# A two-layer decoder on one core: key banks of the first context projection doubled, the folding of layer 1's weights moved to the experts' stage, the stream's row factors made one stage earlier

## The chip, the cores and the metric

The kernel runs on one core of a Trainium2 chip. Its five engines are named as in the profile: PE (TensorE; its weight loads have a row of their own, PEld), DVE (VectorE), ACT (ScalarE), POOL (GpSimd) and SP (SyncE, which here only issues DMAs; its queue is SPq). The metric is the device time of the core in microseconds; less is better.

## The reference

Two decoder layers over a stream `x` of 32 sequences, 112 rows, 256 columns, and a context of 32 times 375 rows of 192 columns:

```
layer 0: x = LN_out(self_attention(LN(x))) * g + b + residual terms     (8 heads of 64)
         x = x + cross_attention(LN(x), context)                        (16 heads of 16, with output projection)
         x = x + top-2-of-8 experts(LN(x))                              (gelu, 1024 hidden)
layer 1: x = x + gated attention(LN(LN(x)*ln_g + ln_b))                 (one head of 128, gate of 512)
         x = x + cross_attention(LN(x)*g + b, LN(context)*tg + tb)      (16 heads of 16)
         x = x + top-2-of-8 experts(x)                                  (squared relu, 512 hidden)
```

Layer 1 normalises with a scale and a shift per column (`ln_g`, `ln_b`, `norm_g`, `norm_b`, `tnorm_g`, `tnorm_b`). The kernel doesn't apply them to the data: it multiplies the scale into the rows of the weights behind the normalisation, and adds the shift times the weights to the bias. This is called the folding. It needs the weights once, at any time before layer 1.

## The kernel before

Seven stages run one after the other, with a barrier of all engines between two of them. Each engine has its own program, and the order in it is written out by hand; engines wait for one another by counting semaphores (`pe.wait_ge(k_low, ...)`). The stages are `self_attention`, `project_context`, `cross_attention` (layer 0), `experts` (layer 0), `gated_attention`, `cross_attention` (layer 1) and `experts` (layer 1).

**project_context.** For each of the 32 contexts (index i) the functions of `context_writer` make the keys and values of layer 0. SP loads the transposed context into one of four slots `ctxT` (three DMAs, L893 and L895). PE multiplies (`project`, L953 to L962): two starts of the values (L953), the keys of two halves m = 0, 1 (L956, L958) and the rest of the values (L959, L960, L962). The keys go to the two PSUM banks `KEYS`, one for each m. ACT copies each key bank into `halves`, rounded (L996, counted by `k_high`), DVE writes the rest that the rounding lost beside it (L1037, counted by `k_low`); ACT and DVE each copy a part of the values into `v` (L1001, L1042). SP stores `halves` (L905, after `k_low`) and `v` (L909), and then loads context i + 4. `halves` and `v` have two slots; ACT and DVE wait for the store of context i - 2 before they write. The values have two pairs of PSUM banks, but the keys have one pair: before the keys of context i, PE waits until DVE has read those of context i - 1 (`pe.wait_ge(k_low, ONE + 2 * i)`).

Beside this the stage does other work, at fixed i. ACT finishes the self-attention's output of two sequences at each of i = 2 to 17 (`move`: four activations, L1090 and L1092). DVE, after its part of i = 4, 6, ..., 18, works on four sequences (`finish`: three adds or products of 1024 columns, L1126 to L1128, and four sets of row statistics, L254). At i = 22 (`ASK`) DVE makes the mean and the row factor of the context for layer 1 (`make_rstd_dve`, 14 small operations with one square root on ACT between them). PE does its part of the folding after context 6 (`fold_pe`: products of the shift with the weights, L339 to L356, into banks 0 and 1), and DVE its part at i = 22 behind the row factors (`fold_dve`: five additions to biases, L365 to L370, and nine products of weights, L373 to L380).

**cross_attention, layer 0.** ACT first clears two slots of `qP` (`clear`, L1426), DVE makes the mean and row factor of the stream `x` (the same 14 operations, on 32 columns) and a tile of ones (L1519), and then for the first two sequences: DVE normalises (L1524), PE turns it (L1301), ACT copies (L1437), PE projects the query (L1307), DVE splits it (L1532 to L1539), SP stores it and loads it back (L1249, L1260), after which the scores (L1325) begin. Keys and values are loaded by L1235 and L1243.

**experts, layer 0.** First comes the routing: PE turns the rows and makes the gate's products, DVE picks two experts for each row and works out the slot of each (a chain of small operations); for this PE counts with two products (L1801, L1802), and later adds up 128 one-hot products in four parts (L1809), each of which waits for DVE's `spread`. DVE reads the result off into the lists `came` and `goes` (L1990 to L2000), and POOL gathers the first rows (L1664). Then the tiles run, 31 of 256 slots and 4 of 128 (`tile`, PE L2103 and L2115; DVE only adds a bias, L2162, and scatters are POOL's). At last a stage part joins the experts' results to `x` and makes the keys and values of layer 1 with `context_writer` (tiles `d_...`; there PE turns the context itself, L938).

Of the kernel before, what the change touches and what calls it, by code (L numbers as in the profile page):

```python
# [20 lines left out]
P = 128  # L21
EPS = 1e-5
GROUP = 4
ONE = 1
# [30 lines left out]
def decoder(nc, d, out):  # L55
# [21 lines left out]
    with ctx:  # L77
# [256 lines left out]
        def fold_pe(pe, wide_ready, folded_ps):  # L334

            pe.wait_ge(later, later_n)
            pe.wait_ge(wide_ready, KD + 2)
            for k in range(KD):
                pe.matmul(bank[1][0:T, :], w.ln_b_wide[:, k, :], w.in_[:, k, 512:1024],  # L339
                          start=(k == 0), stop=(k == KD - 1))  # L340
            for m in range(9):
                for k in range(KD):
                    pe.matmul(bank[0][:, m:m + 1], w.in_[:, k, m * P:(m + 1) * P],
                              w.ln_gb[:, KD + k:KD + k + 1], start=(k == 0), stop=(k == KD - 1))

            for m in range(KD):
                for k in range(KD):
                    pe.matmul(bank[0][:, 16 + m:17 + m], xa[1].wqh[:, k, m, :],
                              xa[1].gb[:, KD + k:KD + k + 1], start=(k == 0), stop=(k == KD - 1))
                for k in range(2):  # L350
                    n = P if k == 0 else C1
                    pe.matmul(bank[0][:, 32 + m:33 + m], xa[1].wkh[0:n, k, m, :],
                              xa[1].gb[0:n, 6 + k:7 + k], start=(k == 0), stop=(k == 1))
            for k in range(2):
                n = P if k == 0 else C1
                last = pe.matmul(bank[0][0:T, D:2 * D], xa[1].b_wide[0:n, 2 + k, 0:T], xa[1].wv[0:n, k, :],  # L356
# [3 lines left out]
        FOLDS = 6 + 4 * KD  # L360

        def fold_dve(dve, fold_chain):

            fold = Chain(dve, fold_chain, 0, FOLDS)
            fold(dve.tensor_tensor(w.b_in_v[:], w.b_in_v[:], bank[1][0:T, :], ALU.add))  # L365
            fold(dve.tensor_tensor(w.b_in_u[:], w.b_in_u[:], bank[0][:, 0:9], ALU.add))
            fold(dve.scalar_tensor_tensor(out=xa[1].bq[:], in0=xa[1].bq[:], scalar=XD ** -0.5,
                                          in1=bank[0][:, 16:16 + KD], op0=ALU.mult, op1=ALU.add))
            fold(dve.tensor_tensor(xa[1].bk[:], xa[1].bk[:], bank[0][:, 32:32 + KD], ALU.add))
            fold(dve.tensor_tensor(xa[1].post[:], xa[1].post[:], bank[0][0:T, D:2 * D], ALU.add))  # L370

            for k in range(KD):
                fold(dve.tensor_scalar(w.in_[:, k, :], w.in_[:, k, :], w.ln_gb[:, k:k + 1], None, ALU.mult))  # L373
                n = P if k == 0 else C1
                wqh, wkh, wv = (xa[1].wqh[:, k].rearrange("c h n -> c (h n)"),
                                xa[1].wkh[:, k].rearrange("c h n -> c (h n)"), xa[1].wv[0:n, k, :])
                fold(dve.tensor_scalar(wqh, wqh, xa[1].gb[:, k:k + 1], None, ALU.mult))
                fold(dve.tensor_scalar(wkh, wkh, xa[1].gb[:, 4 + k:5 + k], None, ALU.mult))
                fold(dve.tensor_scalar(wv, wv, xa[1].gb[0:n, 4 + k:5 + k], None, ALU.mult))
            fold(dve.tensor_scalar(xa[1].wv_twice[:], xa[1].wv_twice[:], xa[1].gb[:, 5:6], None, ALU.mult))  # L380
            fold.close()
# [74 lines left out]
        env.fold_wide, env.fold_pe, env.fold_dve, env.FOLDS = fold_wide, fold_pe, fold_dve, FOLDS  # L456
# [395 lines left out]
def context_writer(e, layer, first, n, tag, sb):  # L852
# [6 lines left out]
    TURN, KEYS = (bank[0], bank[1]), (bank[2], bank[3])  # L859
    V02, V1 = (bank[4], bank[5]), (bank[6], bank[7])  # L860
# [22 lines left out]
    c = Parts()  # L883

# [57 lines left out]
    def project(pe, i):  # L942
# [11 lines left out]
        pe.wait_ge(k_low, ONE + 2 * i)  # L954
        for m, rows in enumerate((low, top)):
            pe.matmul(KEYS[m][:, 0:NKV], a.wkh[rows, 1, m, :], cT[rows, 1, :], start=True, stop=False)  # L956
        for m in range(2):
            pe.matmul(KEYS[m][:, 0:NKV], a.wkh[:, 0, m, :], cT[:, 0, :], start=False, stop=True).then_inc(k_ps, 1)  # L958
# [25 lines left out]
    def scalar(act, i):  # L984
# [7 lines left out]
        for m in range(2):  # L992
# [3 lines left out]
            act.activation(halves[:, i % 2, m, 0, 0:NKV], KEYS[m][:, 0:NKV], ACT.Identity,  # L996
# [1544 lines left out]
```

## Time and profile before

| | us |
|---|---|
| time, median of 3 runs | 2876.21 (2872.34 to 2879.39) |
| the profiled execution's own time | 2876.75 |
| span of the profiled execution | 2874.9 |
| of it `project_context`, from the end of self-attention to the first operation of cross-attention | 384.6 to 573.0 |
| of it the start of cross-attention, to the first scores | 573.0 to 590.5 |
| of it the routing of layer 0 | 1048.0 to 1129.3 |
| PE busy in the span | 2575.8 (90%) |

A row of the timeline gives start, duration, engine, line, operation, output and input, a count, and in brackets the idle time of the engine before it with what ended it. A matmul of 32-bit numbers is two instructions in the trace, so `x4` in a row is two matmuls of the program. A window's row gives for each engine the busy time, then the granted TensorE clock (1.00 is 2.4 GHz, 0.50 is 1.2 GHz), the busy share of the DMA engines and the rate. That share can come out somewhat above 1.

### The profile page before, as it was taken

What the parts mean: (1) busy time and instruction counts of PE and PEld (TensorE: products, weight loads), DVE (VectorE), ACT (ScalarE), POOL (GpSimd) and SP (SyncE); (2) the same over time, 40 slices, a digit from 0 to 9 for tenths busy, and PEclk for the clock granted to TensorE, in tenths of its full rate; (3) what the DMA queues carried; (4) which work ended last, traced back from release to release, by engine and by line L of the source; (5) the groups of instructions that cost most, each with busy time, mean ns of one, the idle gap of its engine ahead of it and who ended that gap; (6) DMA issues with size and microseconds to landing.
All of it is one profiled execution on the core that took longest, in us unless ns stands there. A gap on an engine that the chain in (4) does not pass through costs nothing. (4 is left out here: it accounts for less than half of the span.)

```text
span 2874.9 us, 57394 instructions
## 1 busy us (share of the span) xinstructions
PE 2575.8 (90%) x19210; PEld 2037.6 (71%) x19210; DVE 1529.1 (53%) x3357; ACT 1122.1 (39%) x2398; POOL 599.6 (21%) x652
## 2 busy tenths in 40 slices
PE   7999979789999975999999799899799999579992
PEld 4555555478888864888888566566688888468881
DVE  6777756456766664000000288455577777643334
ACT  2333345345555540333333244222455555312220
POOL 0000000023333310222222100000233333125542
PEclk9999999989999987999999899899899999779995
DMA  5110157777777732555555699000588888226666
GB/s 146 45 29 25 29 174 263 273 194 192 186 189 190 188 93 74 192 192 192 192 192 188 191 343 308 29 1 1 136 204 209 204 203 206 73 93 210 206 208 188
DMA packets 288417, 463.56 MB, mean 161 GB/s; under 512 B 75074, under 2 KB 216228, under 8 KB 288276
## 3 DMA queue, kind: packets, MB, share of 16 engines
q1 hardware_dynamic: 271508, 412.45, 50.3%
q0 software_dynamic: 16768, 49.30, 5.3%
q8 instruction: 80, 1.31, 0.2%
q14 instruction: 61, 0.50, 0.1%
HBM read 342.60 MB, written 119.02 MB: 161 GB/s over the span
## 5 line engine op out<-in xcount | busy, mean ns | idle before, releaser
L1444 ACT ACTIVATE x_probT<-banks 125x448 f32<-125x448 f32 x768 | 418.0, 544 | 382.9 <-PE banks L1341 372.8
L1544 DVE TENSOR_REDUCE x_neg_max<-banks 112x2 f32<-112x750 f32 x512 | 455.4, 930 | 93.4 <-PE banks L1325 93.4
L2103 PE MATMUL banks<-f_xT,f_w 128*128 128x256 f32 (+1 forms) x1680 | 369.9, 377 | 21.8 <-DMA f_b<-in_L_ffn_b 8.6
L2103 PEld LDWEIGHTS banks<-f_xT,f_w 128*128 128x128 f32 x1680 | 310.6, 197 | 74.9 <-issue 11.1
L1490 POOL TENSOR_TENSOR x_diag<-ident,x_neg_max 112x448 fp32r<-112x448 f32 x256 | 240.9, 941 | 581.6 <-DVE x_neg_max L1544 550.6
L2115 PE MATMUL banks<-f_w,f_hT 128*128 128x256 f32 x1584 | 355.8, 381 | 0.0
L1339 PE MATMUL banks<-x_diag,x_ones 112*125 112x448 f32 x768 | 324.0, 422 | 0.7 <-ACT x_probT L1444 0.6
L2115 PEld LDWEIGHTS banks<-f_w,f_hT 128*128 128x128 f32 x1584 | 297.7, 192 | 37.6
L1341 PEld LDWEIGHTS banks<-x_qP,x_kP 128*125 128x125 f32 x1536 | 290.5, 189 | 14.9
L1341 PE MATMUL banks<-x_qP,x_kP 128*125 128x224 f32 x1536 | 290.6, 271 | 0.0
L2162 DVE TENSOR_TENSOR f_y<-banks,f_b 128x256 f32<-128x256 f32 x66 | 25.1, 420 | 475.7 <-PE banks L2115 475.7
L1325 PE MATMUL banks<-x_kP,x_qP 128*112 128x376 f32 x1024 | 264.5, 341 | 9.4 <-DMA x_qP<-q_halves 8.6
L2055 POOL DMA_INDIRECT y_rows<-f_y,f_goes x132 | 131.4, 996 | 465.9 <-DVE f_y L2162 338.3
L2137 ACT ACTIVATE f_hT<-banks,f_b 128x256 f32<-128x256 f32 (+1 forms) x280 | 126.0, 461 | 220.2 <-PE banks L2103 202.7
L1357 PE MATMUL banks<-x_probT,x_v 125*32 125x112 f32 x6144 | 200.2, 263 | 0.8 <-ACT x_o4T L1452 0.8
L1339 PEld LDWEIGHTS banks<-x_diag,x_ones 112*125 112x125 f32 x768 | 143.6, 187 | 32.2 <-ACT x_probT L1444 22.0
L1357 PEld LDWEIGHTS banks<-x_probT,x_v 125*32 125x32 f32 x6144 | 138.6, 109 | 29.9 <-ACT x_o4T L1452 1.2
L1325 PEld LDWEIGHTS banks<-x_kP,x_qP 128*112 128x112 f32 x1024 | 147.1, 180 | 11.8 <-issue 9.1
L2046 POOL DMA_INDIRECT f_x_slots<-x_rows,f_came x124 | 121.6, 980 | 48.9 <-issue 36.6
L2140 ACT ACTIVATE f_hT<-banks 128x256 f32<-128x256 f32 (+1 forms) x140 | 51.9, 371 | 189.1 <-PE banks L2103 188.3
L2154 DVE TENSOR_TENSOR f_hT<-f_hT 128x256 f32<-128x256 f32 (+1 forms) x140 | 57.5, 411 | 88.7 <-ACT f_hT L2140 88.5
L1497 POOL TENSOR_TENSOR x_res<-x_res,x_post 112x256 f32 (+1 forms) x64 | 52.3, 818 | 223.8 <-DVE x_xn L1524 223.8
(331 smaller groups left out, 3789.1 us busy)
## 6 DMA issues: line engine op xcount, KB each, us to landing
x_kP<-k_halves SPq DMA_DIRECT2D x512, 188.0 KB, 3.6
f_w<-in_L_ffn_w SPq DMA_DIRECT2D x70, 1024.0 KB
f_w<-in_L_ffn_w SPq DMA_DIRECT2D x70, 512.0 KB
x_qP<-q_halves SPq DMA_DIRECT2D x512, 56.0 KB, 3.2
x_v<-v_rows SPq DMA_DIRECT2D x64, 408.0 KB, 3.2
k_halves<-p_halves SPq DMA_DIRECT2D x32, 752.0 KB, 4.5
k_halves<-f_d_halves SPq DMA_DIRECT2D x32, 752.0 KB, 6.4
q_halves<-x_q_halves SPq DMA_DIRECT2D x64, 224.0 KB, 2.3
```

The lines of the kernel that those rows point to most:

```text
L1325: last = pe.matmul(bank[2 * pair + k][0:T, 0:NKV + 1], qP[:, s, k, 2 * q + pair, :], kP[:, r, 2 * q + pair, :], start=True, stop=True)
L1339: pe.matmul(to, ones[:], diag[:, u % RING].rearrange("t h k -> t (h k)"), start=True, stop=False)
L1341: last = pe.matmul(to[:, 2 * pair * T:2 * (pair + 1) * T].rearrange("k (h t) -> k h t", t=T), kP[:, r, 2 * q + pair, keys], qP[:, s, :, 2 ...
L1357: last = pe.matmul(PV[j * VW:(j + 1) * VW, 0:T], v[0:KB, s % 2, at:at + VW], probT[:, u % 2, c, j, :], start=(c == 0), stop=(c == NJ - 1))
L1444: act.activation(probT[:, u % 2, c].rearrange("k h t -> k (h t)"), ST[i % 2][0:KB, 0:HU * T], ACT.Exp).then_inc(exp_done, 1)
L1490: pool.tensor_tensor(diag[:, u % RING], wide(ident[0:T, 0:T].unsqueeze(1), 1, HU), wide(mx[:, u % RING, :].unsqueeze(2), 2, T), ALU.mult). ...
L1544: dve.tensor_reduce(mx[:, u % RING, 2 * pair:2 * pair + 2], psum[0:T, 2 * pair:2 * pair + 2, 0:NKV], AX_X, ALU.max, negate=True).then_inc( ...
L2046: pool.indirect_dma_start(out=x_slots[:, n % 2, j, :], out_offset=None, in_=e.x_rows, in_offset=bass.IndirectOffsetOnAxis(ap=came[:, at:at ...
L2055: pool.indirect_dma_start(out=e.y_rows, out_offset=bass.IndirectOffsetOnAxis(ap=goes[:, at:at + 1], axis=0), in_=y[:, n % 2, j, :], in_off ...
L2103: last = pe.matmul(bank[1 + f % 3][:, 0:width], w1[:, r, k, f * P:(f + 1) * P], xT[:, r, k, 0:width], start=(k == 0), stop=(k == KD - 1))
L2115: last = pe.matmul(bank[4 + 2 * r + j][:, 0:D], hT[:, f, j * P:(j + 1) * P], w2[:, r, f, :], start=(f == 0), stop=(f == NF - 1))
L2137: act.activation(hT[:, f, 0:width], bank[1 + f % 3][:, 0:width], ACT.Gelu, bias=b1[:, r, f:f + 1]).then_inc(h_raw, 1)
```

## The change

Four things are done. (1) In layer 0's `context_writer` the keys use four banks, 0 to 3: context i takes one pair, context i + 1 the other, and PE waits for `k_low` of context i - 2 instead of i - 1. (2) `fold_pe` no longer runs in `project_context`; in the routing of layer 0 it stands between the counting products and the one-hot products and writes banks 1 and 2. (3) `fold_dve` is cut in two: the five additions to biases (`fold_biases`) stand at the end of DVE's routing program, and the nine products of weights (`fold_weight`) are put, two for each tile, ahead of DVE's work in tiles 30 to 34 of layer 0's experts. (4) The mean and row factor of the stream for cross-attention of layer 0 are made in `project_context` at i = 26 (`X_ASK`) and no longer at the start of cross-attention. POOL's `fold_wide` stays where it was.

```
     TURN, KEYS = (bank[0], bank[1]), (bank[2], bank[3])
+    if layer == 0:
+        KEYS = bank[0:4]
...
+    def keys_of(i, m):
+
+        return KEYS[(2 * i + m) % len(KEYS)][:, 0:NKV]
...
-        pe.wait_ge(k_low, ONE + 2 * i)
+        pe.wait_ge(k_low, ONE + least(2 * i + 2 - len(KEYS)))
         for m, rows in enumerate((low, top)):
-            pe.matmul(KEYS[m][:, 0:NKV], a.wkh[rows, 1, m, :], cT[rows, 1, :], start=True, stop=False)
+            pe.matmul(keys_of(i, m), a.wkh[rows, 1, m, :], cT[rows, 1, :], start=True, stop=False)
...
-        MOVE, FOLD, ASK = 2, 6, 22
+        MOVE, ASK, X_ASK = 2, 22, 26
...
                 for i in range(B):
                     c.tensor(pe, i)
-                    if i == FOLD:
-                        e.fold_pe(pe, wide_ready, folded_ps)
...
                     if i == ASK:
                         e.make_rstd_act(act, c_std, c_asked, ctmp)
+                    if i == X_ASK:
+                        e.make_rstd_act(act, x_std, x_asked, e.norm_tmp)
...
                         e.make_rstd_dve(dve, chain, c_std, c_asked, e.cmv, e.crstd[:], ctmp, False, e.cstat, e.DC)
-                        dve.wait_ge(folded_ps, 1)
-                        e.fold_dve(dve, fold_chain)
+                    if i == X_ASK:
+                        dve.wait_ge(rested, 3 * NG)
+                        chain = Chain(dve, x_chain)
+                        e.make_rstd_dve(dve, chain, x_std, x_asked, mv, rstd[:], e.norm_tmp, False, e.stat6)
...
-                chain = Chain(dve, pre)
-                e.make_rstd_dve(dve, chain, std_ready, std_asked, mv, rstd[:], e.norm_tmp, layer == 1, e.stat6)
+                if layer == 1:
+                    e.make_rstd_dve(dve, Chain(dve, pre), std_ready, std_asked, mv, rstd[:], e.norm_tmp, True,
+                                    e.stat6)
...
+        FOLD = (bank[1], bank[2])
...
                     pe.wait_ge(xT_ready, ONE + NG * KD)
+                    if layer == 0:
+                        e.fold_pe(pe, FOLD, fold_ps)
                     for n in range(2 * B):
...
                     link(dve.tensor_copy(goes[:], spare[:]))
+                    if layer == 0:
+                        dve.wait_ge(fold_ps, 1)
+                        e.fold_biases(dve, FOLD, Chain(dve, fold_chain))
...
                     width = halves(n) * P
+                    if layer == 0 and type(n) is int:
+                        for j in range(2 * (n - PAIRED + 1), min(e.SCALES, 2 * (n - PAIRED + 2))):
+                            e.fold_weight(dve, j, scale)
```

PE's program after context 6 of `project_context`, before (rows are instructions by line, output, input, shape and count; L953 is the first line of a context, the 128x1 products are the folding of shifts into biases):

```order
L962 MATMUL banks<-x_wv,p_ctxT 125x256 x2
L339 MATMUL banks<-w_in,w_ln_b_wide 112x512 x2
L343 MATMUL banks<-w_ln_gb,w_in 128x1 x18
L348 MATMUL banks<-x_gb,x_wq_by_head 128x1 x2
L352 MATMUL banks<-x_gb,x_wk_by_head 128x1 x2
L348 MATMUL banks<-x_gb,x_wq_by_head 128x1 x2
L352 MATMUL banks<-x_gb,x_wk_by_head 128x1 x2
L356 MATMUL banks<-x_wv,x_b_wide 112x256 x2
L953 MATMUL banks<-x_wv_twice,p_ctxT 125x256 x2
```

Now, in PE's program of the routing of layer 0 (L1821 and L1822 are the two counting products, L1831 the one-hot products; lines of the changed kernel):

```order
L1821 MATMUL banks<-f_both,f_before 112x256
L1822 MATMUL banks<-f_both,f_ones 112x256
L337 MATMUL banks<-w_in,w_ln_b_wide 112x512 x2
L341 MATMUL banks<-w_ln_gb,w_in 128x1 x18
L346 MATMUL banks<-x_gb,x_wq_by_head 128x1 x2
L350 MATMUL banks<-x_gb,x_wk_by_head 128x1 x2
L346 MATMUL banks<-x_gb,x_wq_by_head 128x1 x2
L350 MATMUL banks<-x_gb,x_wk_by_head 128x1 x2
L354 MATMUL banks<-x_wv,x_b_wide 112x256 x2
L1831 MATMUL banks<-f_is_line,f_is_column 66x128 x64
```

The 30 matmuls of the folding have left the middle of `project_context` and stand between the counting and the one-hot products.

DVE's program at i = 22 of `project_context`, before, from the last of the context's row factors to the two key operations of context 23:

```order
L421 TENSOR_TENSOR context_rstd<-p_ctmp 125x96
L365 TENSOR_TENSOR w_b_in_v<-w_b_in_v,banks 112x512
L366 TENSOR_TENSOR w_b_in_u<-w_b_in_u,banks 128x9
L367 SCALAR_TENSOR_TENSOR x_bq<-x_bq,banks 128x2
L369 TENSOR_TENSOR x_bk<-x_bk,banks 128x2
L370 TENSOR_TENSOR x_post<-x_post,banks 112x256
L373 TENSOR_SCALAR w_in<-w_in,w_ln_gb 128x1152
...
L380 TENSOR_SCALAR x_wv_twice<-x_wv_twice,x_gb 128x256
L1037 SCALAR_TENSOR_TENSOR p_halves<-banks,x_bk,p_halves 128x375 x2
```

Now, DVE's program in the last tiles of layer 0's experts (L2193 is the bias of a tile's result, one row for each half of 128 slots):

```order
L378 TENSOR_SCALAR w_in<-w_in,w_ln_gb 128x1152
L381 TENSOR_SCALAR x_wq_by_head<-x_wq_by_head,x_gb 128x256
L2193 TENSOR_TENSOR f_y<-banks,f_b 128x256 x2
L384 TENSOR_SCALAR x_wk_by_head<-x_wk_by_head,x_gb 128x256
L387 TENSOR_SCALAR x_wv<-x_wv,x_gb 128x256
L2193 TENSOR_TENSOR f_y<-banks,f_b 128x256
L378 TENSOR_SCALAR w_in<-w_in,w_ln_gb 128x1152
L381 TENSOR_SCALAR x_wq_by_head<-x_wq_by_head,x_gb 128x256
L2193 TENSOR_TENSOR f_y<-banks,f_b 128x256
```

Between the row factors and the keys of context 23 nothing is left; the products of weights stand ahead of the results of single tiles.

## Rows read from the trace of the kernel before

**Rows 1.** Window of project_context: PE, PEld, DVE, ACT, POOL busy, clock, DMA share, GB/s.

```profile
384.60:573.00 188.40, 161.19 (x700) 102.98 (x700) 103.24 (x235) 86.57 (x163) 1.40 (x4) 0.93 0.80 268
```

**Rows 2.** Waits in project_context: total us, times, longest us.

```profile
PE banks L956 <- DVE p_halves L1037: 15.7, 9, 7.0
```

**Rows 3.** Timeline of PE in project_context: first lines of contexts, and key waits.

```profile
396.31 0.70 PE L953 MATMUL banks<-x_wv_twice,p_ctxT 64*125 64x256 f32 x4
...
419.92 0.70 PE L953 MATMUL banks<-x_wv_twice,p_ctxT 64*125 64x256 f32 x4
...
442.13 0.70 PE L953 MATMUL banks<-x_wv_twice,p_ctxT 64*125 64x256 f32 x4
...
497.71 0.70 PE L953 MATMUL banks<-x_wv_twice,p_ctxT 64*125 64x256 f32 x4
...
507.88 0.70 PE L953 MATMUL banks<-x_wv_twice,p_ctxT 64*125 64x256 f32 x4
...
521.22 0.70 PE L953 MATMUL banks<-x_wv_twice,p_ctxT 64*125 64x256 f32 x4
528.90 1.62 PE L956 MATMUL banks<-p_ctxT,x_wk_by_head 64*128 64x375 f32 x4 [6.99 <-DVE p_halves L1037]
...
535.43 0.70 PE L953 MATMUL banks<-x_wv_twice,p_ctxT 64*125 64x256 f32 x4
...
562.10 0.70 PE L953 MATMUL banks<-x_wv_twice,p_ctxT 64*125 64x256 f32 x4
```

**Rows 4.** Timeline of SP: key stores (L905) and second context loads (L895).

```profile
512.40 0.59 SPq L905 DMA_DIRECT2D k_halves<-p_halves  x1
...
514.90 2.37 SPq L895 DMA_DIRECT2D p_ctxT<-in_ctx_T  x2
517.32 0.59 SPq L905 DMA_DIRECT2D k_halves<-p_halves  x1
...
566.17 0.38 SPq L905 DMA_DIRECT2D k_halves<-p_halves  x1
```

**Rows 5.** Windows with busy DMA: project_context, and layer 1's contexts in experts.

```profile
505.00:520.00 15.00, 15.00 (x67) 9.70 (x66) 7.26 (x19) 5.90 (x12) 0.00 (x0) 1.00 1.02 336
1660.00:1760.00 100.00, 100.00 (x509) 69.89 (x508) 87.15 (x236) 47.39 (x98) 6.57 (x10) 1.00 1.04 339
```

**Rows 6.** DMA issues: queue, count, KB each, median us to landing.

```profile
k_halves<-p_halves SPq DMA_DIRECT2D x32, 752.0 KB, 4.5
k_halves<-f_d_halves SPq DMA_DIRECT2D x32, 752.0 KB, 6.4
```

**Rows 7.** Timeline, start of cross-attention, layer 0: ACT's rows, DVE's normalisation.

```profile
573.04 3.28 ACT L1426 ACTIVATE x_qP<-ident 128x1792 fp32r<-128x1792 f32 x2 [5.79 <-PEq L102]
...
577.90 0.41 DVE L1524 TENSOR_SCALAR x_xn<-x_res,x_mean_var,x_rstd 112x256 f32<-112x256 f32 x1
...
579.03 0.36 ACT L1437 ACTIVATE x_xnT<-banks 128x224 f32<-128x224 f32 x1 [2.59 <-PE banks L1301]
```

**Rows 8.** Timeline of PE in the routing of layer 0.

```profile
1076.32 1.06 PE L1802 MATMUL banks<-f_both,f_ones 112*112 112x256 f32 x2
1096.16 9.40 PE L1809 MATMUL banks<-f_is_line,f_is_column 112*66 112x128 f32 x64 [18.78 <-DVEq L1985]
1109.19 9.71 PE L1809 MATMUL banks<-f_is_line,f_is_column 112*66 112x128 f32 x64 [3.63 <-DVEq L1985]
```

**Rows 9.** Window in the second half of PE's folding: clock.

```profile
434.00:437.00 3.00, 3.00 (x11) 2.21 (x12) 0.00 (x0) 0.00 (x0) 0.00 (x0) 0.50 0.00 0
```

**Rows 10.** Timeline, end of the routing: DVE's last operation, POOL's last gather.

```profile
1120.98 0.20 DVE L2000 CAST f_goes<-f_spare 128x66 uint32<-128x66 f32 x1
...
1125.33 0.95 POOL L1664 DMA_INDIRECT f_x_slots<-x_rows,f_came  x1 [0.30 <-issue]
```

**Rows 11.** Timeline of DVE: end of tile 31 of layer 0's experts.

```profile
1588.59 0.42 DVE L2162 TENSOR_TENSOR f_y<-banks,f_b 128x256 f32<-128x256 f32 x1 [6.49 <-PE banks L2115]
```

**Rows 12.** Timeline of DVE: the largest product of the folding.

```profile
523.31 0.82 DVE L373 TENSOR_SCALAR w_in<-w_in,w_ln_gb 128x1152 f32<-128x1152 f32 x1
```

More of the change, by code:

```diff
@@ L342, in fold_pe @@
                 for k in range(KD):
-                    pe.matmul(bank[0][:, m:m + 1], w.in_[:, k, m * P:(m + 1) * P],
+                    pe.matmul(banks[0][:, m:m + 1], w.in_[:, k, m * P:(m + 1) * P],
                               w.ln_gb[:, KD + k:KD + k + 1], start=(k == 0), stop=(k == KD - 1))
@@ L347, in fold_pe @@
                 for k in range(KD):
-                    pe.matmul(bank[0][:, 16 + m:17 + m], xa[1].wqh[:, k, m, :],
+                    pe.matmul(banks[0][:, 16 + m:17 + m], xa[1].wqh[:, k, m, :],
                               xa[1].gb[:, KD + k:KD + k + 1], start=(k == 0), stop=(k == KD - 1))
@@ L351, in fold_pe @@
                     n = P if k == 0 else C1
-                    pe.matmul(bank[0][:, 32 + m:33 + m], xa[1].wkh[0:n, k, m, :],
+                    pe.matmul(banks[0][:, 32 + m:33 + m], xa[1].wkh[0:n, k, m, :],
                               xa[1].gb[0:n, 6 + k:7 + k], start=(k == 0), stop=(k == 1))
@@ L355, in fold_pe @@
                 n = P if k == 0 else C1
-                last = pe.matmul(bank[0][0:T, D:2 * D], xa[1].b_wide[0:n, 2 + k, 0:T], xa[1].wv[0:n, k, :],
+                last = pe.matmul(banks[0][0:T, D:2 * D], xa[1].b_wide[0:n, 2 + k, 0:T], xa[1].wv[0:n, k, :],
                                  start=(k == 0), stop=(k == 1))
             last.then_inc(folded_ps, 1)
[L360 to L366, printed above, removed]
-            fold(dve.scalar_tensor_tensor(out=xa[1].bq[:], in0=xa[1].bq[:], scalar=XD ** -0.5,
[L368 to L372, printed above, removed]
-                fold(dve.tensor_scalar(w.in_[:, k, :], w.in_[:, k, :], w.ln_gb[:, k:k + 1], None, ALU.mult))
[L374 to L381, printed above, removed]
@@ L995, in scalar @@
                 act.wait_ge(k_stored[i % 2], 16 * (i // 2))
-            act.activation(halves[:, i % 2, m, 0, 0:NKV], KEYS[m][:, 0:NKV], ACT.Identity,
+            act.activation(halves[:, i % 2, m, 0, 0:NKV], keys_of(i, m), ACT.Identity,
                            bias=a.bk[:, m:m + 1]).then_inc(k_high, 1)
@@ L2011, in experts @@
         down_ps = count("down_ps")
+        scaled = flag("scaled")
         e.start_counts()
```

47 lines of the change are left out of this document (37 added, 10 removed).

## The prediction, written before the changed kernel was timed

> **What bounds the kernel now.** I read the stages first by windows, since the change touches three of the seven. Over the whole span PE is busy 90%, but this mean says nothing of a stage. In project_context PE is busy 161.2 of 188.4 us, at a clock of 0.93 and with the DMA engines at 0.80 [rows 1]. The second view is the waits of project_context: PE waited nine times, 15.7 us, before the keys (L956) for DVE's reading of the key banks (L1037), and one of these waits was 7.0 us long [rows 2]. The third is PE's timeline, by the starts of L953, the first line of a context. Without a wait a context takes 4.445 us: (562.10 - 535.43) / 6 [rows 3]. From context 1 (396.31) to context 31 (562.10) 165.8 us pass, where 30 contexts without a wait are 133.35 us: 32.4 us are lost [rows 3]. They have three parts:
> - PE's folding. Contexts 6 and 7 together, 419.92 to 442.13, take 22.2 us; a pair with one key wait takes 10.17 us elsewhere (497.71 to 507.88) and context 6 has a wait a little longer, so I count 10.3. The folding costs 11.9 us [rows 3]. Its last part ran at half clock (0.50 [rows 9]), and this is in it.
> - DVE's row factors and folding at i = 22: the context that starts at 521.22 ends at 535.43, 14.2 us instead of 4.445, so 9.8 us. Of this 6.99 us are the wait at L956; the rest is the slow clock after it (L956 took 1.62 us at 528.90) [rows 3].
> - What is left of the 32.4, 10.7 us, is in the eight other key waits, about 1.3 us each: 10.17 for two contexts instead of 8.89 [rows 3]. They stand where DVE or ACT had other work between two contexts.
>
> **Part 1 and 2, project_context.** The folding leaves PE and DVE there, so the first part and most of the second go at once. With four key banks PE waits for DVE one context later than now, so DVE may be late by 4.445 us more before PE feels it. Eight of the nine waits were about 1.3 us and vanish under that; of the ninth, 6.99 us, 2.5 us would stay if DVE's folding stayed, but it goes. PE's floor is the full 32.4 us less.
>
> What is late next? The DMAs. A context moves 752 KB of keys [rows 6], 408 KB of values and 375 KB of loads (187.5, and 93.8 twice), 1.572 MB. At 4.445 us for each this would be 354 GB/s. The highest sustained rate in the trace is 339 GB/s over 100 us, in the same kind of work for layer 1, at a DMA share of 1.04, and there a key store takes 6.4 us to land instead of 4.5 [rows 5, 6]. From 505 to 520 project_context itself moved 336 GB/s at 1.02 [rows 5], and there SP fell behind: the second context load held it for 2.37 us and its key stores were 4.92 us apart (512.40, 517.32) while PE went on at 4.445 [rows 4]. So the full DMA sets the pace, through SP and through ACT's and DVE's wait for the store of context i - 2. I take 1.572 MB / 339 GB/s = 4.64 us for a context; the ends are 4.445 us (PE alone, nothing lost to DMA) and 4.92 us (SP's longest interval).
>
> The sum goes by key stores. One comes 4.07 us after its context's L953 (562.10 to 566.17 [rows 3, 4]), so that of context 1 stays at 400.4. Then 26 contexts with loads at 4.64 us, 120.6 us, lead to 521.0, and the last four, which have no loads, take 4.445 us each, 17.8 us: the last key store is issued at 538.7 instead of 566.17. That is 27.4 us less; by the ends 32.4 and 20.1 us.
>
> The Trainium skill ("DMA: Bandwidth & Descriptors", Specifications) gives about 358 GB/s as the limit of one core's way to HBM. An estimate by this page would be 4.39 us for a context, under PE's 4.445, and the 32.4 us would come whole; the trace, whose highest long window is 339 GB/s at a share over 1 [rows 5], does not bear it out, but no window here asked for more.
>
> **Part 3, the folding in the routing.** PE ends the counting products at 1077.4 and then waits 18.78 us for DVE's first one-hot tiles [rows 8]. The 30 matmuls fall into this gap. They took 11.9 us of PE's time before, partly at half clock. In the routing PE is idle before them and at the low level, so twice that, 23.8 us, is the upper bound: they end between 1089.3 and 1101.2. The one-hot products that could start at 1096.16 take 9.4 us, and the next batch can't start before 1109.19, since DVE has nothing ready [rows 8]. At worst PE ends the first batch at 1110.6 and is 1.4 us late; at best the PE comes to the one-hot products with a higher clock and gains about 1 us in the second batch. I take nothing: the middle, 1095.3, is before 1096.16. DVE's five additions stand behind its last list, at 1121.2; none is longer than the largest product of the folding, 0.82 us [rows 12], so they end by 1125.3, and POOL's gathers run to 1126.3 and hide them [rows 10]. The nine products of weights, at most 0.82 us each [rows 12] and 1.6 us for a tile, stand where DVE had been idle for 6.49 us [rows 11]. Cost: nothing. If the cover were gone it would be up to 7.4 us for all nine.
>
> **Part 4, the row factors of the stream.** At the start of cross-attention DVE normalised at 577.90 and ACT copied at 579.03, 1.13 us later [rows 7]. Without the 14 operations DVE normalises less than 0.5 us after the stage's start, and PE's product is there by 574.7. But ACT's two clears run from 573.04 to 576.32 [rows 7], and they now end last: the copy starts at 576.3. That is 2.7 us less, not the 4.5 of DVE's chain, and everything up to the first scores follows that copy. In project_context the 14 operations at i = 26 take DVE no more than the 4.9 us that they took here (573.0 to 577.90); with the doubled banks PE doesn't wait for them, and without this cover they would cost about 1.3 us, as DVE's other work between two contexts does.
>
> **The sum.** 27.4 + 2.7 = 30.1 us off the profiled execution's own 2876.75 us; this lies 0.5 us above the median, so I predict 2846.1 us.
>
> **The rivals.**
> - *The DMA keeps up.* PE goes at 4.445 us in all contexts: 32.4 + 2.7 = 35.1 us, 2841.1 us. For it: from 535.43 on PE had no wait although the contexts came at this pace [rows 3]. Against it: SP's intervals of 4.92 us and the share of 1.02 [rows 4, 5]. The page's 358 GB/s says this. 17%.
> - *The key banks bring little.* If the waits were only the sign of ACT, DVE or SP being full, the two foldings would go and the pairs stay near today's pace: 11.9 + 9.8, less the 1.3 us that the row factors at i = 22 keep, plus 2.7, is 23.1 us, 2853.1 us. SP at 4.92 us gives nearly the same: 20.1 + 2.7 = 22.8. For it: in the pairs with `finish` DVE and ACT are each busy for most of the time. Against it: the waits named in rows 2 are on the banks. 16%.
> - *The folding lies on the routing's path.* PE and DVE are slower than I count and the one-hot products wait for all of it: the forecast plus 1.4 to 5 us, about 2850. 4%.
> - *Slower: the stores' round trip takes the place of the bank.* ACT writes `halves` of context i only when the store of i - 2 has landed. A full DMA lengthens the landing, and a pair of contexts can't be shorter than a landing and the time in which ACT and DVE fill the slot again, some 2 us of the 4.07 from L953 to the store. To end more than 0.3% above the median, the last key store would have to come at 577.5, so 6.1 us for each of the 26 contexts and a landing of over 10 us each time. The medians are 4.5 and 6.4 us [rows 6]. 2%.
> - *No difference,* if what project_context gains were lost again at a slower pace of the loads, 5.8 us for a context. 1%.
>
> **How the numbers follow.** The forecast has 60%. Its own range, from a pace of 4.55 to 4.75 us, is 2844 to 2849. To hold 8 in 10 the range must reach to both neighbours, 2841.1 and 2853.1, and 1.5 to 3 us beyond for the spread of medians (the three runs of before lie within 7 us): 2839.5 to 2855. A measurement of this kernel tells about 0.3%, 8.6 us, from no change. Faster by more than that are the first three cases and the forecast, 97%; the same 1%; slower 2%.
>
> **What would show it.** In the profile of the changed kernel: PE has no wait for DVE's L1037 line in project_context; the key stores are about 4.64 us apart between contexts 3 and 27, with a DMA share near 1 and 335 to 345 GB/s; ACT or SP now wait for landings; the stage ends near 545 instead of 573. The first copy of cross-attention (L1437 before) follows the clears at once, about 16.5 us or less before the first scores. PE's one-hot products in the routing start 19 to 20 us after the counting products end, as before. The prediction is wrong if the pace is not set by the DMAs, above all if PE goes at 4.445 us throughout or if pairs of contexts with `finish` still take 10 us.

## The result, and the profile after

The changed kernel takes 2845.04 us (median of 3 runs, 2839.32 to 2848.01) where the kernel before takes 2876.21: a ratio of 0.9894, with an interval of 0.9875 to 0.9912. The profiled execution is itself 2845.04 us long, with a span of 2843.3. The forecast was 2846.1 us, in a range of 2839.5 to 2855.

First the waits in the middle of `project_context` (lines of before have moved: L1009, before L996, is ACT's key copy, L1050 DVE's, L966 to L975 are PE's products of a context, L918 and L922 SP's two stores). From 398 to 540, columns: total us, times, longest us.

```profile
DVE p_halves L1050 <- ACT p_halves L1009: 41.1, 20, 3.9
ACT p_halves L1009 <- DMA k_halves<-p_halves: 36.9, 21, 4.1
```

PE's nine waits for DVE [rows 2] are gone, and nothing took their place on PE. What waits now is ACT, 21 times, for the landing of the key store of context i - 2, and DVE behind it. PE's timeline, first lines of contexts 1 and 31:

```profile
396.00 0.70 PE L966 MATMUL banks<-x_wv_twice,p_ctxT 64*125 64x256 f32 x4
...
529.35 0.70 PE L966 MATMUL banks<-x_wv_twice,p_ctxT 64*125 64x256 f32 x4
```

That is 133.35 us for 30 contexts, exactly PE's 4.445 us each, against 165.79 before [rows 3]. The windows (of the stage, and of its part in which context loads are still issued: PE, PEld, DVE, ACT, POOL, clock, DMA share, GB/s) and SP's timeline at the stage's end:

```profile
384.60:543.70 159.10, 145.26 (x640) 93.11 (x640) 98.60 (x235) 85.06 (x164) 1.40 (x4) 0.96 0.95 317
400.00:525.00 125.00, 125.00 (x565) 80.35 (x563) 87.94 (x203) 75.80 (x148) 0.00 (x0) 1.00 1.00 337
403.00:525.00 122.00, 122.00 (x551) 78.69 (x549) 85.72 (x197) 74.85 (x147) 0.00 (x0) 1.00 1.02 343
```

```profile
525.32 0.58 SPq L918 DMA_DIRECT2D k_halves<-p_halves  x1
526.00 0.44 SPq L922 DMA_DIRECT2D v_rows<-p_v  x1
527.63 0.38 SPq L918 DMA_DIRECT2D k_halves<-p_halves  x1
528.43 1.01 SPq L922 DMA_DIRECT2D v_rows<-p_v  x1
532.04 0.38 SPq L918 DMA_DIRECT2D k_halves<-p_halves  x1
532.52 0.44 SPq L922 DMA_DIRECT2D v_rows<-p_v  x1
535.88 0.38 SPq L918 DMA_DIRECT2D k_halves<-p_halves  x1
536.36 0.45 SPq L922 DMA_DIRECT2D v_rows<-p_v  x1
543.77 1.40 SPq L1251 DMA_DIRECT2D x_kP<-k_halves  x3
```

The whole rate was 268 GB/s at a share of 0.80 [rows 1] and is 317 at 0.95; with loads it is 337 GB/s at 1.00, and 343 at 1.02 from 403 on, when the store of context 1 is out. The last key store comes 6.5 us after its L966 (535.88 - 529.35), where before it came 4.07 us after [rows 3, 4], and the next stage begins 7.9 us after it (before 6.85). PE goes at its own pace, and the stores lag behind it. The lag can be followed:

```profile
402.14 0.39 SPq L918 DMA_DIRECT2D k_halves<-p_halves  x1
...
410.46 0.60 SPq L918 DMA_DIRECT2D k_halves<-p_halves  x1
...
520.84 0.60 SPq L918 DMA_DIRECT2D k_halves<-p_halves  x1
```

```profile
516.01 0.70 PE L966 MATMUL banks<-x_wv_twice,p_ctxT 64*125 64x256 f32 x4
```

The first three are the key stores of contexts 1, 3 and 27 (SP), the last is PE's start of context 28. The stores of contexts 1 to 28 came (525.32 - 402.14) / 27 = 4.56 us apart, PE's contexts 4.445: the lag grew from 6.1 to 9.3 us. The start of this stretch belongs to another engine, though. Context 1's store is late in the kernel before too, by 6.2 us, when DVE works on the row factors of the self-attention's output:

```profile
402.54 0.39 SPq L905 DMA_DIRECT2D k_halves<-p_halves  x1
```

From context 3 to 27, the stretch that the prediction names, the stores came (520.84 - 410.46) / 24 = 4.60 us apart, and 4.65 and 4.64 us in the two other profiles of this kernel. The last three stores, with no context loads beside them, came 3.52 us apart and made up 2.8 us of the lag.

At the start of cross-attention ACT's first copy (L1454) now follows the two clears (L1442) at once, 3.2 us after the stage's start instead of 6.0 [rows 7]; but PE's first scores start 16.1 us after the stage's start (before 17.5):

```profile
543.79 3.28 ACT L1442 ACTIVATE x_qP<-ident 128x1792 fp32r<-128x1792 f32 x2 [8.03 <-PEq L102]
546.98 0.34 ACT L1454 ACTIVATE x_xnT<-banks 128x224 f32<-128x224 f32 x1
```

```profile
559.90 0.63 PE L1341 MATMUL banks<-x_kP,x_qP 128*112 128x376 f32 x1 [5.81 <-DMA x_qP<-q_halves]
```

In PE's timeline of the routing the folding (L337 to L354) stands in the gap of rows 8:

```profile
1045.99 1.06 PE L1822 MATMUL banks<-f_both,f_ones 112*112 112x256 f32 x2
1046.84 3.48 PE L337 MATMUL banks<-w_in,w_ln_b_wide 128*112 128x512 f32 x4
1050.16 4.66 PE L341 MATMUL banks<-w_ln_gb,w_in 128*128 128x1 f32 x36
...
1058.42 2.32 PE L354 MATMUL banks<-x_wv,x_b_wide 128*112 128x256 f32 x4
1065.75 9.52 PE L1831 MATMUL banks<-f_is_line,f_is_column 112*66 112x128 f32 x64 [5.01 <-DVEq L2007]
```

It ends at 1060.7, after 13.9 us; 5.0 us of the gap are left. The one-hot products start 19.76 us after the counting product L1822, before 19.84 [rows 8].

I profiled the changed kernel three times and the kernel before twice, so that the stretches of one program can be told from their spread. All in us, from the timelines:

| stretch | before | after | difference of means |
|---|---|---|---|
| start to context 1 on PE | 396.3, 396.1 | 396.0, 396.6, 397.5 | +0.5 |
| context 1 to 31 on PE | 165.8, 165.7 | 133.4, 133.5, 134.0 | -32.1 |
| context 31 to the end of the stage | 10.9, 10.9 | 14.4, 15.2, 14.3 | +3.7 |
| from there to the first scores | 17.5, 17.5 | 16.1, 16.2, 16.3 | -1.3 |
| first scores to the gate's products | 465.9, 465.3 | 466.1, 465.7, 465.3 | +0.1 |
| gate's products to the first tile | 74.8, 75.2 | 74.9, 75.1, 75.0 | 0.0 |
| first tile to layer 1's contexts | 502.0, 501.3 | 501.4, 501.8, 501.6 | 0.0 |
| from there to the end | 1241.8, 1241.8 | 1241.0, 1237.0, 1241.2 | -2.1 |

Stages that nothing in the change touches vary by up to 4 us in the last stretch of the table, and from 1234.6 to 1243.9 us over the profiles of all variants below. So a difference of 1 to 3 us is read from its own stretch below, not from the whole time.

### The profile page after: what moved, and what is told of

The parts are those of the page before. It is cut to its first block and busy times, and to the rows that moved or that the text cites. A ratio compares the mean times of both kernels' runs of the same rounds, so it can differ in the third digit from the quotient of the medians.

```text
span 2843.3 us, 57393 instructions
## 1 busy us (share of the span) xinstructions
PE 2573.2 (90%) x19210; PEld 2038.3 (72%) x19210; DVE 1529.3 (54%) x3357; ACT 1121.4 (39%) x2398; POOL 599.8 (21%) x652
## 5 line engine op out<-in xcount | busy, mean ns | idle before, releaser
L2193 DVE TENSOR_TENSOR f_y<-banks,f_b 128x256 f32<-128x256 f32 x66 | 25.1, 420 | 470.4 <-PE banks L2141 470.4
```

## The experiments

**The kernel itself again**, twice, beside its variants.

> The changed kernel itself, once more beside its variants, to know how far two profiles of one program differ in each stretch. Both theories: about 2845 us, contexts of project_context at 4.445 us on PE, key stores at 4.56 us between contexts 1 and 28, 7 to 8 us from the last key store to the next stage, 16.1 us from there to the first scores. Stretches that differ by more than 0.5 us from the first profile can't carry an argument of a microsecond.

> The changed kernel a third time, beside the variant that is to beat it. Both theories: 2845 to 2847 us; first scores 16.1 us after the start of cross-attention, gate products 482 us after it.

2846.55 us (ratio 0.9905, 0.9890 to 0.9920) and 2843.77 us (0.9887, 0.9872 to 0.9902), in the stretches of the table. In the third profile PE waited once in `project_context` for DVE's `p_v` line, 0.6 us: the lag of the stores just reaches PE there. Of the eight profiles with four key banks, all loads and all products, here and below, four have such waits, each 0.6 to 1.5 us in sum.

**One pair of key banks.**

```
     TURN, KEYS = (bank[0], bank[1]), (bank[2], bank[3])
-    if layer == 0:
-        KEYS = bank[0:4]
```

> Only the keys of layer 0 go back to one pair of banks. Theory A (the key banks were a real wait): the eight steps where DVE does its rows make PE wait about 1.3 us each again, 10.7 us, and the row factors at i = 22 and i = 26 no longer have their cover and cost about 1.3 us each: +12 to +13 us, 2857 to 2858 us, and PE's waits for DVE's key line come back, ten of them. Theory B (the wait was only the sign of ACT, DVE or the DMAs being full): the time stays within 3 us of the changed kernel's, and the pairs of contexts with extra work take as long with four banks as with two.

2855.25 us (0.9933, 0.9919 to 0.9947), 8.7 us more than the changed kernel beside it on the same chip. Its waits in the stage, and key waits in PE's timeline:

```profile
PE banks L967 <- DVE p_halves L1048: 10.3, 10, 1.3
```

```profile
402.10 0.90 PE L967 MATMUL banks<-p_ctxT,x_wk_by_head 64*128 64x375 f32 x4 [1.12 <-DVE p_halves L1048]
...
460.39 0.70 PE L964 MATMUL banks<-x_wv_twice,p_ctxT 64*125 64x256 f32 x4
462.10 0.90 PE L967 MATMUL banks<-p_ctxT,x_wk_by_head 64*128 64x375 f32 x4 [1.01 <-DVE p_halves L1048]
466.12 0.70 PE L964 MATMUL banks<-x_wv_twice,p_ctxT 64*125 64x256 f32 x4
...
511.50 0.90 PE L967 MATMUL banks<-p_ctxT,x_wk_by_head 64*128 64x375 f32 x4 [0.82 <-DVE p_halves L1048]
```

Ten waits, as many as theory A has, but not all where it has them. Eight follow DVE's work on the rows (contexts 6, 8, ..., 20) and one the row factors at i = 22 (context 24, at 511.50). The tenth is at context 2 (402.10), behind the row factors of the self-attention's output, and the row factors that were moved to i = 26 make PE wait nowhere, with one pair of banks as with two. Most such contexts take 5.73 us instead of 4.445 (all lie between 5.54 and 5.97), so ten cost 13 us, and from context 1 to 31 PE takes 146.3 us, 12.7 more than the mean of the changed kernel. From context 1 to the stage's end it is only 158.1 us against 148.3, 9.8 more: after context 31 the stage ends in 11.8 us instead of 14.7. With the waits back the DMAs have time again (313 GB/s at 0.94 from 400 to 520) and the lag of the stores is gone. Theory B falls. The banks bring 9.8 us, what they take off PE less what the fuller DMAs take back. It also sizes the rest: against the kernel before, this variant's stage is 18.6 us shorter from context 1 to its end (176.7 to 158.1). That is, within 0.2 us, the two foldings (11.9 + 9.8), less the wait that the row factors at i = 22 keep (1.1), less a wait at context 8 that the folding had covered (1.3), less an end that is 0.9 us longer.

**The context loads left out.**

```
+        if layer == 0 and i >= LOADS:
+            return
...
-            pe.wait_ge(ctx_loaded[i % LOADS], 16 * SHARES * (i // LOADS + 1))
+            pe.wait_ge(ctx_loaded[i % LOADS], 16 * SHARES)
```

> In layer 0 only the first four contexts are loaded and used for all 32 (the output is that of repeated contexts); all products, copies and stores stay. The DMA demand of a context falls from 1.572 to 1.197 MB (750 KB... that is, keys 752 KB and values 408 KB stay of it, 1.16 MB with padding), at 4.445 us about 265 GB/s. Theory A (the full DMAs set the pace of the stores, PE's 4.445 us is just under it): the key stores follow at 4.445 us, landings of key stores fall back to 4.5 us or less, and the stage ends 1 to 2 us earlier, from the lag of the stores and a shorter drain. Theory B (the prediction's step: DMAs at 339 GB/s cost 4 to 5 us over the stage): 4 to 5 us less. Theory C (the DMAs don't matter): less than 0.5 us, key stores still at 4.56 us.

The demand is in fact 1.188 MB for a context: keys of 752 KB and values of 408 KB, a KB of the profile being 1024 bytes. At 4.445 us for each that is 267 GB/s, and the window shows just that. The time is 2844.41 us (0.9885, 0.9865 to 0.9905). The window with few loads, then the landings of the issues from 400 to 530 (queue, count, KB each, median us), here and in the changed kernel:

```profile
400.00:520.00 120.00, 120.00 (x542) 77.15 (x541) 88.27 (x204) 75.03 (x147) 0.00 (x0) 1.00 0.73 267
```

```profile
k_halves<-p_halves SPq DMA_DIRECT2D x30, 752.0 KB, 3.6
```

```profile
k_halves<-p_halves SPq DMA_DIRECT2D x29, 752.0 KB, 5.3
p_ctxT<-in_ctx_T SPq DMA_DIRECT2D x27, 187.5 KB, 5.3
```

PE's 30 contexts take 133.35 us again. PE's first line of a context is L968 here. The key stores no longer lag: they follow it by 4.07 us where DVE has no other work, at context 28 and at the last (529.37 to 533.44), and ACT has no wait for a landing. The stage ends 11.8 us after context 31 instead of 14.7: 2.9 us less. So the DMAs cost the stage about 3 us, through the lag and not through PE's pace: between theory A (1 to 2) and B (4 to 5) in size, A in mechanism. Theory C falls. The share says something too: 267 GB/s at 0.73 would be 366 GB/s at a share of 1 (an estimate), where the changed kernel has 337 at 1.00. So by this measure a byte of the context loads takes more of the DMAs' time than a byte of the stores. The whole time doesn't show the 3 us, its last part being 1244 us this time.

**Fewer products on PE, and both cuts at once.**

```
...
-        pe.matmul(values[0], cT[:, 0, 0:KB], a.wv[:, 0, :], start=False, stop=True)
-        for k in range(2):
+        if layer == 1:
+            pe.matmul(values[0], cT[:, 0, 0:KB], a.wv[:, 0, :], start=False, stop=True)
+        for k in range(2 if layer == 1 else 1):
...
```

Two products are left out in layer 0, the second of the first value bank and the second of the third, not three as the next text says: a context has 16 matmul instructions in the trace instead of 20. The rest of the edit ends the sums in these banks one product earlier.

> In layer 0 three products of the values are left out (the second term of the first value bank and one term of the third), so PE's own time for a context falls from 4.445 to about 3.8 us; the transfers stay as they are. Theory A (the DMAs are now full, 1.572 MB for each context): PE soon waits for context loads or for banks, contexts stay at 4.4 to 4.5 us, that is 350 GB/s, and the stage is at most 2 us shorter. Theory B (PE alone is the bound and the DMAs have room): the contexts go at 3.9 to 4.1 us and the stage is 10 us or more shorter. Theory C (ACT or DVE, each with some 3.4 us of work for a context and 4.3 to 4.7 where they have extra work, is next): between the two, and in the steps with extra work PE waits for them.

> Both cuts at once: the three products of the values are left out in layer 0, and only the first four contexts are loaded. Theory A (in the run with fewer products alone the full DMAs kept the contexts at 4.42 us): with 1.16 MB for each context PE's shorter work now shows, contexts without extra work come 3.6 to 3.9 us apart, 30 of them take 110 to 122 us instead of 132.7. Theory B (the cut products were no bound of PE's, or ACT and DVE held the contexts at 4.4 us): 130 us or more.

With fewer products alone: 2843.99 us (0.9895, 0.9879 to 0.9912). PE's contexts, 1 and 31, and the window:

```profile
393.74 0.70 PE L966 MATMUL banks<-x_wv_twice,p_ctxT 64*125 64x256 f32 x4
...
526.39 0.70 PE L966 MATMUL banks<-x_wv_twice,p_ctxT 64*125 64x256 f32 x4 [0.94 <-DMA p_ctxT<-in_ctx_T]
```

```profile
400.00:520.00 120.00, 103.50 (x431) 60.39 (x430) 85.30 (x197) 74.02 (x145) 0.00 (x0) 0.94 1.01 340
```

132.65 us for 30 contexts, 4.42 each: the cut takes more off PE than I had estimated (context 1 takes 3.58 us, 393.74 to 397.32, and not 3.8), yet 30 contexts gain 0.7 us. The waits from 398 to 530:

```profile
ACT p_halves L1012 <- DMA k_halves<-p_halves: 40.6, 25, 3.2
PE banks L966 <- DVE p_v L1058: 15.1, 11, 2.6
...
PE banks L966 <- DMA p_ctxT<-in_ctx_T: 2.3, 4, 0.9
```

DVE's part of the values (L1058) stands behind ACT's wait for the key stores, so I read both as the DMAs'. The stores of contexts 1 to 28 came 4.53 us apart ((523.17 - 400.84) / 27), and 4.55 us from context 3 to 27, where the changed kernel has 4.60; and from context 1 to the stage's end it is 148.2 us against 148.3. With both cuts 30 contexts take 118.4 us (398.38 to 516.76), 3.95 each, inside theory A's range, at a DMA share of 0.80 from 400 to 500; the whole was 2833.23 us in its one run. So less work on PE shows where the DMAs have room, and with the loads the DMAs hold the stage: theory A. Theory C, ACT or DVE as the bound, falls with it, since both had the same work in the 118.4 us. The 3.95 us are still more than PE's 3.58: PE waits 8.3 us for DVE's `p_v` line, and ACT 25 us for landings of key stores. While loads run, the stores' own floor is about 4.55 us, 2.4% above PE's 4.445. Whether a third slot of `halves` would lower it was not tried; the share of 1.01 speaks against it.

**The row factors back in cross-attention** (ACT's part is shown; DVE's goes back in the same way, and at i = 26 nothing is left):

```
-                if layer == 1:
-                    e.make_rstd_act(act, std_ready, std_asked, e.norm_tmp)
+                e.make_rstd_act(act, std_ready, std_asked, e.norm_tmp)
```

> Only the mean and row factor of the stream go back to the start of cross-attention. Theory A (the prediction: everything up to the first scores follows ACT's first copy): +2.7 us, first scores 18.8 us after the stage's start instead of 16.1. Theory B (read from the changed kernel's profile: the first query store is issued 2.8 us earlier, but takes 3.9 us to land instead of 2.4, because the first key loads and the last stores of project_context are still under way): the store is issued 2.8 us later again but lands faster, first scores about 17.4 us after the start, +1.3 us. Theory C (nothing of it reaches the scores): 0.

2847.93 us (0.9914, 0.9899 to 0.9930). First scores 18.4 us after the stage's start (543.57 to 562.01), 2.3 us more than in the changed kernel: nearer to theory A than to B, but 1.0 us more than the kernel before with the same program there. SP's timeline of the first query here, in the kernel before, and in the changed kernel (L1259 and L1249 store the query, L1270 and L1260 load it back; in the changed kernel L1265 and L1276):

```profile
553.23 0.39 SPq L1259 DMA_DIRECT2D q_halves<-x_q_halves  x1
553.66 1.55 SPq L1253 DMA_DIRECT2D x_v<-v_rows  x1
556.59 0.79 SPq L1270 DMA_DIRECT2D x_qP<-q_halves  x2
```

```profile
582.69 0.39 SPq L1249 DMA_DIRECT2D q_halves<-x_q_halves  x1
583.12 0.51 SPq L1243 DMA_DIRECT2D x_v<-v_rows  x1
585.06 3.56 SPq L1260 DMA_DIRECT2D x_qP<-q_halves  x8
```

```profile
550.61 0.39 SPq L1265 DMA_DIRECT2D q_halves<-x_q_halves  x1
551.04 0.50 SPq L1259 DMA_DIRECT2D x_v<-v_rows  x1
554.48 3.56 SPq L1276 DMA_DIRECT2D x_qP<-q_halves  x8
```

From store to load are 3.36 us, 2.37 (in the second profile 2.36) and 3.87 us. So ACT's copy comes 2.8 us earlier by the change, and the query's way through memory takes 1.5 us of it again. In this run the last key load had landed 0.6 us before the store was issued, and the way still took 3.36 us.

**The query ahead of the second half of the keys, and the copy ahead of the clears.**

```
-                for half in range(2):
-                    load_keys(0, 0, half)
+                load_keys(0, 0, 0)
...
-                load_values(0, 0)
...
+                load_keys(0, 0, 1)
+                load_values(0, 0)
```

(The first stands ahead of the first query's store in SP's program, the second, `load_values`, stood between its store and its load, and the last stands behind both. The order is changed in both cross-attentions. In the second variant ACT's `clear(s)` also stands behind `copy_xT(0, s)`, s = 0, 1.)

> At the start of both cross-attentions SP issues the loads of the second half of the keys and of the values behind the store and load of the first query instead of ahead of it. Theory A (the first key and value loads slow down the landing of the query store): the store lands in 2.4 us instead of 3.9, the load likewise, and the first scores come 14.6 us after the stage's start instead of 16.1: 1.5 us less in layer 0. Theory B (it is project_context's last stores that are still under way): no change. Theory C (the keys' second half is then late): the scores of the second half wait, and the gain is lost again.

> As the run before it, and in layer 0 ACT copies the first turned rows ahead of each of its two clears. Theory A (the two clears of 3.3 us together are what ends last ahead of the first copy): the copy starts 1.5 to 2 us after the stage's start instead of 3.2, the query goes out 1.3 to 1.7 us earlier, but ACT's second copy waits for a clear: 1 to 1.5 us less than the run before it, some 2.5 us less than the changed kernel in all. Theory B: the loads' landing absorbs it as it absorbed half of the gain of the row factors: less than 0.5 us.

> The variant with the first query ahead of the second half of the keys, and the first copies ahead of the clears, once more. Theory A (its first profile is typical): first scores 13.6 us after the stage's start instead of 16.1, gate products 478.4 us after it instead of 482, and 2.5 to 3.7 us less in the whole, which five rounds may not tell from nothing. Theory B (the first profile was a lucky one): the gate products come 481 us or later after the stage's start.

With the query first: 2844.47 us (0.9898, 0.9881 to 0.9914); store to load 3.08 us instead of 3.87 and first scores at 15.4 us, so 0.8 us less where theory A had 1.5; the four key loads that were left ahead had landed 1.6 us before the store. With the copy ahead of the clears too: 2845.0 us (0.9895, 0.9878 to 0.9911) and 2845.66 (0.9898, 0.9880 to 0.9916).

```profile
545.70 0.36 ACT L1455 ACTIVATE x_xnT<-banks 128x224 f32<-128x224 f32 x1 [9.33 <-PE banks L1317]
545.95 1.69 ACT L1442 ACTIVATE x_qP<-ident 128x1792 fp32r<-128x1792 f32 x1
550.37 0.36 ACT L1455 ACTIVATE x_xnT<-banks 128x224 f32<-128x224 f32 x1 [2.73 <-PE banks L1317]
```

The copy starts 1.35 us after the stage's start, and the first scores at 13.6 and 12.8 us against 16.1 to 16.3: 3.0 us less. The gate's products come 478.4 and 478.2 us after the stage's start against 481.6 to 482.3, so theory A holds in its stretch. In the whole time it can't be told from the changed kernel (2843.77 us beside 2845.66 on the same chip), and I don't claim that it is faster.

**The folding left out**, with its five additions (`fold_biases`), which are cut in the same way.

```
-                    if layer == 0:
-                        e.fold_pe(pe, FOLD, fold_ps)
...
-                        for j in range(2 * (n - PAIRED + 1), min(e.SCALES, 2 * (n - PAIRED + 2))):
-                            e.fold_weight(dve, j, scale)
```

> PE's folding in the routing, the five additions and the nine products of weights are left out (layer 1 then lacks its folded scales and shifts). Theory A (all of it is hidden): the time stays within 1 us of the changed kernel's; PE's one-hot products start 20 us after the counting products end with or without the folding, the first tile starts 53 us after them, the tiles' last part is as long. Theory B (a part lies on the routing's path or its half-clock hurts the one-hot products): 1.4 to 5 us less, seen in the stretch between the counting products and the first tile. Theory C (the folding keeps PE's clock up for the one-hot products): 1 us more in the same stretch.

2844.52 us (0.9896, 0.9881 to 0.9911). PE's timeline between the counting and the one-hot products, without the folding:

```profile
1046.08 1.06 PE L1822 MATMUL banks<-f_both,f_ones 112*112 112x256 f32 x2
1065.93 4.29 PE L1829 MATMUL banks<-f_is_line,f_is_column 112*66 112x128 f32 x19 [18.79 <-DVEq L2005]
```

19.85 us between them, against 19.76 with the folding; gate's products to first tile 74.9 us against 74.9 to 75.1; first tile to layer 1's contexts 501.6 against 501.4 to 501.8. The last stretch reads up to 503.7 us in variants that change nothing in it, so a cost under 2 us there is told only by the lowest values, which agree. The folding is hidden in all its parts: theory A. The whole is 2.0 us under the changed kernel beside it, but the stretches that were edited don't hold it.

## Why the prediction was right, and where it was not

- **The floor of PE.** Forecast: 32.4 us come off PE with the folding gone and the banks doubled. Measured 32.1 (table). The waits of rows 2 were real ones, which the run with one pair of banks shows by bringing them back: ten, each of which makes its context 1.1 to 1.5 us longer. One price beside the sum was wrong: the row factors at i = 26 were to cost about 1.3 us without the second pair of banks, and in that run they cost nothing.
- **The DMAs' pace.** Forecast: 4.64 us between key stores, from 339 GB/s. Measured 4.60, 4.65 and 4.64 us in three profiles between contexts 3 and 27, at a share of 1.02 in the first, with nearly the same pace (4.55) when PE has less to do. So the DMAs do set the stores' pace, and the size was right. What I had wrong is that this would slow PE: the prediction calls itself wrong if PE goes at 4.445 us throughout, and PE did, with not one wait. The buffers between PE and the stores (four key banks, two slots of `halves`) take up a lag that grew to 9.3 us, of which the 4.07 us of an undisturbed context are not the DMAs'; 27 contexts are just too few to fill them. In the second profile the lag grew to 10.6 us and PE lost 0.2 us, in the third it grew to 9.7 us and PE waited 0.6 us.
- **The last key store.** Forecast 538.7, measured 535.9, 537.1 and 538.0. For the first of them, by terms: context 1's store came at 402.1 and not at 400.4, since its lag is 6.1 us and not the 4.07 that I took from context 31 (+1.7), which the trace of before showed (402.54); 27 intervals took 123.2 us instead of 125.1 (-1.9), half of it between contexts 1 and 3, where that lag shrinks again; the last three, which I had at 4.445 us, took 3.52, because stores that lag catch up once the loads end (-2.8).
- **The end of the stage.** I counted no change behind the last store; it was 7.9 to 8.3 us instead of 6.85. The full DMAs explain little of that, since it was 7.7 us in the run without loads and in the one with one pair of banks; what does is open. The stage ended 27.9 us earlier in the mean, forecast 27.4: a lag that was partly made up (-) and a longer drain (+) nearly cancel, so that the sum came out better than its terms is luck. The prediction named PE at 4.445 us throughout as a sign that it is wrong; its number holds because the stores at the stage's end paid about what it had charged to PE. Of PE's 32.1 us, 3.7 are given back between context 31 and the end; the run without loads returns 2.9 of them.
- **The rival that the DMA keeps up** came true for PE's pace, not for the stores: they went at 338 to 342 GB/s by bytes and pace (1.572 MB in 4.65 to 4.60 us), and the forecast took 339. The Trainium skill ("DMA: Bandwidth & Descriptors", Specifications) gives about 358 GB/s as the limit. With loads and stores together the runs don't reach it: 345 GB/s with less work on PE is the most that contexts 3 to 27 showed. Short windows of stores alone go above it, 377 GB/s in the run with both cuts:

```profile
480.00:490.00 10.00, 10.00 (x46) 5.67 (x42) 5.39 (x16) 3.27 (x6) 0.00 (x0) 1.00 1.03 377
```

So the figure is too high for this mixture and too low for stores alone, and the windows of the kernel before were nearer.
- **The rival that the banks bring little** falls: they bring 9.8 us of stage time.
- **The row factors.** Forecast -2.7 us, measured -1.3. The step that failed is "everything up to the first scores follows that copy". The copy did come 2.8 us earlier, but the query's store then met the key loads, the last of which landed 8.9 us after the stage's start: 3.87 us from store to load instead of 2.37. Moving half of these loads behind it gave 0.8 us back. The other 0.7 us are not shown to be theirs, since the way took 3.1 to 3.4 us in three runs where those loads had landed or nearly so. Undone alone, the step costs 2.3 us, since the store then took 3.36 us.
- **The folding in the routing.** Forecast 0, measured 0. PE took 13.9 us for it, between the bounds of 11.9 and 23.8 and nearer to the lower, so that it ended 5.0 us ahead of the one-hot products; I had the margin at 0.9. DVE's five additions ran beside POOL's gathers and the products of weights in its idle time.
- **The sum.** -30.1 forecast; -31.2, -28.7 and -31.8 us in three comparisons of medians. Of the terms -27.9 and -1.3 are in the stretches of the change. The last stretch of the table, -2.1 us, is not explained; it varies as much between profiles of one kernel.

## What to carry to other kernels

When a bank or buffer is doubled, work out the next floor, and then how much lag the buffers behind it can hold: here the DMAs' floor (4.60 to 4.65 us) was 3 to 5% above PE's (4.445), and over 27 contexts the buffers took up nearly all of it, so that PE gained 32.1 of 32.4 us and the stage paid 3.7 us at its end, 2.9 of them for stores that lag and land later. Such a stage has nothing more to give on PE alone (a fifth less work for a context, 0.7 us). And a chain shortened ahead of a store moves that store into other traffic: count the landing at its new place. Changes of 1 to 3 us are judged by the stretch they touch, since the whole varies by more.

## What the runs showed of the hardware

- Mixed loads and stores ran at 338 to 342 GB/s by bytes and pace over contexts 3 to 27, and at 345 with less work on PE. Windows agree where they start with the stores: 343 GB/s from 403 to 525. The one from 400 reads 337 because context 1's store comes only at 402.14 (80 GB/s from 400 to 403).
- Without the loads the same share moved more: 267 GB/s at 0.73, and 377 at 1.03 over 10 us, against 343 at 1.02 with them.
- A 752 KB store landed in a median of 3.6 us at 267 GB/s in all, and in 5.3 us at 337 GB/s. ACT's wait for it was nothing in the first case and in the kernel before, and 36.9 us in the changed kernel, of which PE felt none.
- The first query's way from store to load took about 2.4 us (three profiles) or 3.1 to 3.4 us (three others) where the key loads ahead of it had landed or were within a microsecond of it, and 3.6 to 4.3 us (eight profiles) with them still under way. What sets the one or the other of the first two is open; in the run with the row factors moved back the DMA share fell to 0.12 for half a microsecond between two bursts, and nothing was tried on it.
- PE's folding took 13.9 us in the routing at a mean clock of 0.62 (level 1.2 GHz for most of it), and 11.9 us before in `project_context`, where the clock was 0.74 from 426 to 438 and fell to 0.50 [rows 9].
